# Two groups of gathered samples weighted by one multiply and summed by one sum

## The chip, the cores and the metric

One core of one Trainium2 chip runs the whole program in one launch. The metric is the device time in microseconds, the median of three runs. The core has TensorE (PE, matmuls, with its own queue for weight loads), VectorE (DVE), ScalarE (ACT), GpSimd (POOL) and SyncE (SP), which issues most transfers. Each engine takes its instructions in program order; between engines they wait for each other's semaphores.

## The reference

The input `x` has shape (4, 256, 64, 64). Four residual layers follow one another, each `x = x + layer(group_norm(x))`. The change touches the first, a deformable convolution. Cut to that part:

```
G, P = 4, 9                      # groups of 64 channels, sampling points
xp     = inproj(y)               # the table that is sampled, padded by 6
offset = off(t); mask = softmax(mask_lin(t), over the 9 points of a group)
samp   = grid_sample(img, grid)  # 4 corners a point, bilinear
dout   = (samp * mask).sum(over the 9 points)
```

For each pixel and group 9 points x 4 corners = 36 vectors of 64 channels are fetched, each is multiplied by one weight (bilinear weight times mask), and the 36 are added up. The rest of layer 0 is 1x1 convolutions with a squeeze-and-excite gate. Layer 1 is a grouped convolution with rotated kernels, layer 2 linear attention with batch statistics, layer 3 a depthwise-like convolution with quantised weights.

## The kernel before

The four images (b = 0 to 3) go through stages: A (norm, first convolution, table, depthwise convolution, offsets, indices and weights), F (output projection and feed-forward), L1 and L2 (layers 1 and 2). L3, layer 3, comes last for all. The gathers of image b - 1 or b are spread as "units" over the stages that run meanwhile, in the order of the list `plan`.

An image has 32 tiles of 128 pixels (`TILES`), a tile 4 groups (`G`): 512 units in all. For a unit GpSimd issues nine indirect gathers (L430), each of 128 partitions x 4 corners x 64 channels, into one of four places of the buffer `ring`, one place a group. It waits for the semaphore `ring_free` (L426) before a unit: the place must have been summed in the tile before. VectorE's `unit` (L1491) waits for the nine gathers (`gathered0` to `gathered3`), multiplies the place by its weights in place (L1506), waits for that (`weighted`), adds up the 36 vectors into `dbuf` (L1512) and gives the place back. Ahead of a tile's first unit the tile's 144 weights are copied into PSUM (L1495) in the stretches called apart. In the others (the last F and the extra tiles there) the multiply is cut in four and takes its weights from `wt` in SBUF. A tile's `dbuf` is stored by SyncE when all four groups are summed (L490).

Where VectorE's units stand among its other work is fixed when the program is written. `Stream.begin` (L379) lists the units of a turn, `TURNS` says how many tiles a turn takes, `give` (L388) puts the next few at a place in the loop body, and `finish` (L393) the rest at its end. `extra` (L402) puts one whole tile between stages. The places that matter below are these:
- la, the first loop of L2 (L1976), gives two units at a time, four times a turn.
- lb, the second loop of L2 (L2032), gives one unit ahead of a chunk's wait for ScalarE (`bO`) and one behind the chunk. The loop of L1 (L1914) has the same form: two units at a time, but one where it runs as "L1 last".
- f1 (L1774), the first loop of F, gives two units ahead of its first chunk and one behind each chunk. f2 (L1816), the second, gives one unit behind each of eight steps.
- a1 (L1627) and a2 (L1661), the loops of A, give one unit at a time; the depthwise part of a2 gives one behind its fourth and eighth tap.

Stages are parted by barriers of all engines but GpSimd (L327). GpSimd goes on through them, as far as places are free.

Of the kernel before, what the change touches and what calls it, by code (L numbers as in the profile page):

```python
# [20 lines left out]
ALU = mybir.AluOpType  # L21
ACT = mybir.ActivationFunctionType
AX_X = mybir.AxisListType.X
# [5 lines left out]
P = 128  # L29
# [7 lines left out]
TILES = HW // P  # L37
G, K2 = 4, 9
GC = C // G
PTS = G * K2  # L40
CORNERS = 4
# [33 lines left out]
PARTS = 4  # L75
# [59 lines left out]
def network_kernel(nc, x, par, wa, wr, wf, wq, w3, out):  # L135
    ctx = ExitStack()
    with ctx:
        def sb(name, shape, dt=F32):
            return ctx.enter_context(nc.sbuf_tensor(name, shape, dt))
# [6 lines left out]
        def sem(name):  # L146
            if name not in sems:
                sems[name] = ctx.enter_context(nc.semaphore(name))
            return sems[name]
# [15 lines left out]
        ring = sb("ring", [P, G, K2 * CORNERS * GC])  # L165
        idx = sb("idx", [P, 2, TILES * PTS], U32)
        idx_stage = sb("idx_stage", [P, 2, 2 * PTS], U32)
        wt = sb("wt", [P, TILES * PTS * CORNERS])
        dbuf = sb("dbuf", [P, 4, C])
# [9 lines left out]
        wps = PS[:, 7, 0:PTS * CORNERS]  # L179
# [73 lines left out]
        def seg(t, start, n):  # L253
            return t[:, bass.ds(start, n)]
# [1225 lines left out]
        def _(dve):  # L1480
            vec = nc.vector
# [8 lines left out]

            def unit(b, t, g, j):  # L1491

                if g == 0:
                    if stream.apart:
                        vec.tensor_copy(wps, seg(wt, t * (PTS * CORNERS), PTS * CORNERS)).then_inc(sem("wt_moved"), 1)  # L1495
                        dve.wait_ge(sem("wt_moved"), t + (b * TILES + 1))
                    else:
                        dve.sem_inc(sem("wt_moved"), 1)
                dve.wait_ge(sem(f"gathered{g}"), t * (16 * K2) + 16 * K2 * (b * TILES + 1))
                parts = 1 if stream.apart else PARTS  # L1500
                n = K2 * CORNERS // parts
                for part in range(parts):
                    rg = ring[:, g, part * n * GC:(part + 1) * n * GC].rearrange("p (k c) -> p k c", c=GC)
                    weights = wps[:, g * n:(g + 1) * n] if stream.apart \
                        else seg(wt, t * (PTS * CORNERS) + (g * PARTS + part) * n, n)
                    last = vec.tensor_tensor(rg, rg, weights.unsqueeze(2).to_broadcast([P, n, GC]), ALU.mult)  # L1506
                last.then_inc(sem("weighted"), 1)
                dve.wait_ge(sem("weighted"), t * G + (b * TILES * G + g + 1))
                if g == 0:

                    dve.wait_ge(sem("d_stored"), t * 16 + (16 * b * TILES + 16 - 16 * j))
                vec.tensor_reduce(dbuf[:, j, g * GC:(g + 1) * GC], ring[:, g, :].rearrange("p (k c) -> p c k", c=GC),  # L1512
                                  AX_X, ALU.add).then_inc(sem("ring_free"), 1)

            stream = Stream(unit)

            def weights_for(gi, all_tiles=True):
# [772 lines left out]
```

## Time and profile before

| | us |
|---|---|
| runs, median (lowest to highest) | 6932.77 (6926.98 to 6935.47) |
| profiled execution | 6945.93 |
| its span | 6944.1 |
| VectorE busy | 5165.7 (74%) |
| GpSimd busy | 4465.9 (64%) |
| TensorE busy | 3732.4 (54%) |
| ScalarE busy | 1121.1 (16%) |

The span runs from the first instruction to the last; the profiled execution's own time has 1.8 us around it. Busy time leaves out what an engine spends on waits, branches and on issuing: GpSimd shows 64%, although its gathers follow one another closely for most of the span. What an engine waited for stands in brackets behind a row of the timeline.

### The profile page before, as it was taken

How to read it: one execution, taken by the hardware profiler on the slowest of the kernel's cores; microseconds unless marked ns; L12 is line 12 of the kernel's file. 1: busy time of each engine (PE TensorE's matmuls, PEld its weight loads, DVE VectorE, ACT ScalarE, POOL GpSimd, SP SyncE). 2: the span in 40 equal slices, each digit the busy share in tenths (PEclk: the TensorE clock that was granted, in tenths of full speed). 3: DMA queues.
4: the chain of work that ended last, by engine and by line, in shares of the span. 5: the costliest groups of instructions: out<-in, count | busy, mean ns of one | idle time of the engine just before them, and what ended most of it. 6: DMA issues, size and time to landing. Idle time of an engine off the chain costs nothing.

```text
span 6944.1 us, 44944 instructions
## 1 busy us (share of the span) xinstructions
PE 3732.4 (54%) x11426; PEld 1972.3 (28%) x11426; DVE 5165.7 (74%) x4213; ACT 1121.1 (16%) x1689; POOL 4465.9 (64%) x4677
## 2 busy tenths in 40 slices
PE   7243251351574526643874436536747654296969
PEld 4122121221232204421321124312223431143534
DVE  5879788797787768976787679867777996535545
ACT  2010100101111002221110012211110221111335
POOL 0777777777777777777777777777777777500000
PEclk9576675675787758866886668767878877698989
DMA  4463643644444333465443334564343446311048
GB/s 118 141 172 105 192 141 121 207 129 159 144 132 131 106 107 123 131 216 186 130 131 118 107 109 131 194 202 142 120 128 108 129 132 221 127 43 45 37 145 237
DMA packets 529912, 954.28 MB, mean 137 GB/s; under 512 B 268560, under 2 KB 325904, under 8 KB 513680
## 3 DMA queue, kind: packets, MB, share of 16 engines
q0 software_dynamic: 221184, 604.27, 27.9%
q1 hardware_dynamic: 308624, 348.78, 15.5%
q8 instruction: 46, 0.75, 0.0%
q14 instruction: 58, 0.48, 0.0%
HBM read 792.34 MB, written 160.37 MB: 137 GB/s over the span
## 4 chain that ended last, share of the span: by engine, by line
POOL 43%; issue 21%; DVE 15%; PE 13%; DMA 4%; ACT 2%; SPq 1%; DVEq 0%; POOLq 0%; ACTq 0%
POOL ring L430 43%; PE PS L791 13%; DVE ring L1506 5%; DVE dbuf L1512 2%; DMA ring<-table,idx_stage 1%; DMA img<-d_dram 1%; ACT img L1184 1%; DVE sm L1968 1%; DVE sm L1984 1%; DVE sm L1991 0%; DVE img L1937 0%; DVE img L1995 0%; DMA img<-q_dram 0%; SPq L678 0%; DVE wb_sb L2002 0%
## 5 line engine op out<-in xcount | busy, mean ns | idle before, releaser
L430 POOL DMA_INDIRECT ring<-table,idx_stage x4608 | 4442.7, 964 | 1414.8 <-issue 1372.3
L1512 DVE TENSOR_REDUCE dbuf<-ring 128x64 f32<-128x2304 f32 x512 | 2072.6, 4048 | 30.3 <-DMA d_dram<-dbuf 1.8
L791 PE MATMUL PS<-img,wb_sb 128*128 128x512 f32 (+1 forms) x3328 | 1655.7, 657 | 495.0 <-DVE img L1824 251.5
L1506 DVE TENSOR_TENSOR ring<-ring,PS 128x2304 f32<-128x2304 f32 x480 | 1224.4, 2551 | 605.5 <-DMA ring<-table,idx_stage 594.6
L791 PE MATMUL PS<-img,wa_sb 128*128 (+2 forms) x2848 | 842.7, 635 | 603.2 <-DVE img L1920 224.3
L791 PEld LDWEIGHTS PS<-img,wb_sb 128*128 128x128 f32 x3328 | 693.6, 213 | 1424.1 <-issue 1002.2
L791 PEld LDWEIGHTS PS<-img,wa_sb 128*128 128x128 f32 (+1 forms) x2848 | 368.9, 164 | 1047.5 <-issue 983.2
L473 POOL MEMSET img<- 128x6745 f32 x1 | 5.7, 5722 | 719.0 <-DMA o_dram<-img 719.0
L1184 ACT ACTIVATE img<-PS,sm 128x512 f32<-128x512 f32 x384 | 247.8, 680 | 1028.8 <-PE PS L791 1026.6
L791 PE MATMUL PS<-wa_sb,cb 128*128 128x108 f32 (+1 forms) x1024 | 239.3, 400 | 312.9 <-DVE cb L1575 250.4
L791 PE MATMUL PS<-sm,params 128*128 128x4 f32 x28 | 7.7, 350 | 726.9 <-DVE sm L1554 709.1
L888 PE MATMUL PS<-params,img 128*128 128x128 f32 x256 | 62.9, 427 | 543.1 <-DMA img<-d_dram 543.1
L791 PEld LDWEIGHTS PS<-wa_sb,cb 128*128 128x128 f32 x1024 | 214.9, 277 | 356.1 <-DVE cb L1575 262.3
L1184 ACT ACTIVATE img<-PS 128x512 f32<-128x512 f32 (+1 forms) x224 | 173.9, 777 | 718.5 <-PE PS L888 379.1
L1184 ACT ACTIVATE img<-img (+6 forms) x241 | 185.5, 772 | 615.9 <-PE PS L791 297.1
L1824 DVE SCALAR_TENSOR_TENSOR img<-PS,sm,img 128x512 f32<-128x512 f32 x256 | 179.3, 742 | 141.4 <-ACT img L1184 141.4
L1090 PE MATMUL PS<-params,img 128*128 128x128 f32 x512 | 108.3, 392 | 279.9 <-ACT img L1184 245.3
L791 PE MATMUL PS<-cb,img 128*128 128x256 f32 x1024 | 251.0, 395 | 2.0 <-ACT img L1184 2.0
L1184 ACT ACT_TABLE_LOAD x20 | 25.7, 1283 | 1349.2 <-DVE sm L1559 1348.3
L791 PE MATMUL PS<-wb_sb,img 128*128 128x512 f32 x512 | 230.8, 604 | 11.8 <-ACT img L1184 11.6
L791 PEld LDWEIGHTS PS<-sm,params 128*128 128x128 f32 x28 | 6.9, 312 | 734.7 <-issue 734.7
L888 PEld LDWEIGHTS PS<-params,img 128*128 128x128 f32 x256 | 50.2, 224 | 562.1 <-issue 532.7
(223 smaller groups left out, 3379.1 us busy)
## 6 DMA issues: line engine op xcount, KB each, us to landing
ring<-table,idx_stage POOLq DMA_INDIRECT x4608
table<-cb SPq DMA_DIRECT2D x64, 512.0 KB, 5.9
img<-y_dram SPq DMA_DIRECT2D x64, 512.0 KB, 6.4
q_dram<-img SPq DMA_DIRECT2D x32, 1024.0 KB, 4.3
img<-q_dram SPq DMA_DIRECT2D x32, 1024.0 KB, 8.5
img<-in_x SPq DMA_DIRECT2D x8, 2048.0 KB, 12.0
y_dram<-cb SPq DMA_DIRECT2D x64, 256.0 KB, 2.2
d_dram<-dbuf SPq DMA_DIRECT2D x128, 128.0 KB
```

What stands on the lines that cost most here:

```text
L430: nc.gpsimd.indirect_dma_start(out=ring[:, g, p * CORNERS * GC:(p + 1) * CORNERS * GC], out_offset=None, in_=tab[b], in_offset=bass.Indire ...
L473: nc.gpsimd.memset(img2[:, 0:FIRST[3]], 0.0).then_inc(sem("e_cleared"), 1)
L791: return nc.tensor.matmul(o, l, r, start=start, stop=stop, **kw)
L888: last = nc.tensor.transpose(PS[:, 2 * h + k, s * P:(s + 1) * P], i2[h][:, s * C + k * P:s * C + (k + 1) * P], v("ident"))
L1090: last = nc.tensor.transpose(PS[:, m, s * P:(s + 1) * P], QS[:, s * HID + m * P:s * HID + (m + 1) * P], v("ident"))
L1184: return nc.scalar.activation(o, i, f, **kw)
L1506: last = vec.tensor_tensor(rg, rg, weights.unsqueeze(2).to_broadcast([P, n, GC]), ALU.mult)
L1512: vec.tensor_reduce(dbuf[:, j, g * GC:(g + 1) * GC], ring[:, g, :].rearrange("p (k c) -> p c k", c=GC), AX_X, ALU.add).then_inc(sem("ring_ ...
L1824: last = vec.scalar_tensor_tensor(out=i2[6 + q % 2][:, half], in0=PS[:, 2 * (q % 2) + j, :], scalar=fb[:, 2 * q + j:2 * q + j + 1], in1=i2 ...
L1968: link(vec.tensor_reduce(cmax[:, s2], PS[:, s2, :], AX_X, ALU.max))
L1984: link(vec.tensor_reduce(mx, q3, AX_X, ALU.max))
```

## The change

`unit` on VectorE does nothing for groups 0 and 2. For groups 1 and 3 it waits for both gathers, that of the group before and its own, multiplies both places at once (128x4608, or eight instructions of 128x576 where weights come from SBUF), sums both at once into 128 values (two groups of 64) and raises `ring_free` by two. The semaphores' counts are set to match. GpSimd's code is the same: it asks for the same numbers, and the number for the first place of a pair now comes with that of the second.

```diff
@@ -1490,27 +1490,34 @@
 
             def unit(b, t, g, j):
 
-                if g == 0:
+                if g % 2 == 0:
+                    return
+                if g == 1:
                     if stream.apart:
                         vec.tensor_copy(wps, seg(wt, t * (PTS * CORNERS), PTS * CORNERS)).then_inc(sem("wt_moved"), 1)
                         dve.wait_ge(sem("wt_moved"), t + (b * TILES + 1))
                     else:
                         dve.sem_inc(sem("wt_moved"), 1)
-                dve.wait_ge(sem(f"gathered{g}"), t * (16 * K2) + 16 * K2 * (b * TILES + 1))
-                parts = 1 if stream.apart else PARTS
-                n = K2 * CORNERS // parts
-                for part in range(parts):
-                    rg = ring[:, g, part * n * GC:(part + 1) * n * GC].rearrange("p (k c) -> p k c", c=GC)
-                    weights = wps[:, g * n:(g + 1) * n] if stream.apart \
-                        else seg(wt, t * (PTS * CORNERS) + (g * PARTS + part) * n, n)
-                    last = vec.tensor_tensor(rg, rg, weights.unsqueeze(2).to_broadcast([P, n, GC]), ALU.mult)
+                for h in (g - 1, g):
+                    dve.wait_ge(sem(f"gathered{h}"), t * (16 * K2) + 16 * K2 * (b * TILES + 1))
+                both = ring[:, g - 1:g + 1, :]
+                n = K2 * CORNERS
+                if stream.apart:
+                    rg = both.rearrange("p g (k c) -> p (g k) c", c=GC)
+                    last = vec.tensor_tensor(rg, rg, wps[:, (g - 1) * n:(g + 1) * n].unsqueeze(2).to_broadcast([P, 2 * n, GC]), ALU.mult)
+                else:
+                    n = n // PARTS
+                    for part in range(2 * PARTS):
+                        rg = both.rearrange("p g c -> p (g c)")[:, part * n * GC:(part + 1) * n * GC].rearrange("p (k c) -> p k c", c=GC)
+                        weights = seg(wt, t * (PTS * CORNERS) + ((g - 1) * PARTS + part) * n, n)
+                        last = vec.tensor_tensor(rg, rg, weights.unsqueeze(2).to_broadcast([P, n, GC]), ALU.mult)
                 last.then_inc(sem("weighted"), 1)
-                dve.wait_ge(sem("weighted"), t * G + (b * TILES * G + g + 1))
-                if g == 0:
+                dve.wait_ge(sem("weighted"), t * 2 + (b * TILES * 2 + g // 2 + 1))
+                if g == 1:
 
                     dve.wait_ge(sem("d_stored"), t * 16 + (16 * b * TILES + 16 - 16 * j))
-                vec.tensor_reduce(dbuf[:, j, g * GC:(g + 1) * GC], ring[:, g, :].rearrange("p (k c) -> p c k", c=GC),
-                                  AX_X, ALU.add).then_inc(sem("ring_free"), 1)
+                vec.tensor_reduce(dbuf[:, j, (g - 1) * GC:(g + 1) * GC].rearrange("p (g c) -> p g c", g=2),
+                                  both.rearrange("p g (k c) -> p g c k", c=GC), AX_X, ALU.add).then_inc(sem("ring_free"), 2)
 
             stream = Stream(unit)
```

On VectorE, at the start of lb, the second loop of L2, before (L1512 gives one place back, L2038 waits for ScalarE's `bO`):

```order
L2024 COPY wb_sb<-PS 64x4x64
...
L1495 COPY PS<-wt 128x144
...
L1506 TENSOR_TENSOR ring<-ring,PS 128x2304 [waits gathered0]
...
L1512 TENSOR_REDUCE dbuf<-ring 128x64 [waits d_stored]
...
L2038 ISA [waits bO]
L2038 BN_STATS ostats<-PS 128x6
...
L2038 BN_STATS ostats<-PS 128x6
...
L2042 SCALAR_TENSOR_TENSOR img,lm<-img,lm,PS 128x512
...
L2042 SCALAR_TENSOR_TENSOR img,lm<-img,lm,PS 128x512
L1506 TENSOR_TENSOR ring<-ring,PS 128x2304 [waits gathered1]
...
L1512 TENSOR_REDUCE dbuf<-ring 128x64 [waits weighted]
```

The same place after:

```order
L2031 COPY wb_sb<-PS 64x4x64
...
L2045 ISA [waits bO]
L2045 BN_STATS ostats<-PS 128x6
...
L2045 BN_STATS ostats<-PS 128x6
...
L2049 SCALAR_TENSOR_TENSOR img,lm<-img,lm,PS 128x512
...
L2049 SCALAR_TENSOR_TENSOR img,lm<-img,lm,PS 128x512
...
L1497 COPY PS<-wt 128x144
...
L1507 TENSOR_TENSOR ring<-ring,PS 128x4608 [waits gathered1,gathered0]
...
L1519 TENSOR_REDUCE dbuf<-ring 128x128 [waits d_stored]
```

The first group's weight copy, multiply and sum stood ahead of the chunk's work and of its wait for `bO`. Now nothing of the units stands there; the weight copy and the pair come behind the chunk.

On VectorE, in f2, the second loop of F, before (L1824 is a step of the feed-forward):

```order
L1824 SCALAR_TENSOR_TENSOR img<-PS,sm,img 128x512 [waits gD]
...
L1495 COPY PS<-wt 128x144
...
L1506 TENSOR_TENSOR ring<-ring,PS 128x2304 [waits gathered0]
...
L1512 TENSOR_REDUCE dbuf<-ring 128x64 [waits d_stored]
...
L1824 SCALAR_TENSOR_TENSOR img<-PS,sm,img 128x512 [waits gD]
...
L1506 TENSOR_TENSOR ring<-ring,PS 128x2304 [waits gathered1]
...
L1512 TENSOR_REDUCE dbuf<-ring 128x64 [waits weighted]
...
L1824 SCALAR_TENSOR_TENSOR img<-PS,sm,img 128x512 [waits gD,gZ]
...
L1506 TENSOR_TENSOR ring<-ring,PS 128x2304 [waits gathered2]
...
L1512 TENSOR_REDUCE dbuf<-ring 128x64 [waits weighted]
```

The same place after (the step's line is L1831):

```order
L1831 SCALAR_TENSOR_TENSOR img<-PS,sm,img 128x512 [waits gD]
...
L1831 SCALAR_TENSOR_TENSOR img<-PS,sm,img 128x512 [waits gD]
...
L1497 COPY PS<-wt 128x144
...
L1507 TENSOR_TENSOR ring<-ring,PS 128x4608 [waits gathered1,gathered0]
...
L1519 TENSOR_REDUCE dbuf<-ring 128x128 [waits d_stored]
...
L1831 SCALAR_TENSOR_TENSOR img<-PS,sm,img 128x512 [waits gD,gZ]
...
L1831 SCALAR_TENSOR_TENSOR img<-PS,sm,img 128x512 [waits gD,gZ]
...
L1507 TENSOR_TENSOR ring<-ring,PS 128x4608 [waits gathered3,gathered2]
...
L1519 TENSOR_REDUCE dbuf<-ring 128x128 [waits weighted]
```

Groups and steps took turns one by one. Now two steps follow each other, and then a pair.

## Rows read from the trace of the kernel before

**Rows 1.** The page: engines' busy time; shares of the chain that ended last.
```profile
PE 3732.4 (54%) x11426; PEld 1972.3 (28%) x11426; DVE 5165.7 (74%) x4213; ACT 1121.1 (16%) x1689; POOL 4465.9 (64%) x4677
...
POOL 43%; issue 21%; DVE 15%; PE 13%; DMA 4%; ACT 2%; SPq 1%; DVEq 0%; POOLq 0%; ACTq 0%
```

**Rows 2.** The page's costliest groups: busy us, mean ns, then idle before.
```profile
L430 POOL DMA_INDIRECT ring<-table,idx_stage x4608 | 4442.7, 964 | 1414.8 <-issue 1372.3
L1512 DVE TENSOR_REDUCE dbuf<-ring 128x64 f32<-128x2304 f32 x512 | 2072.6, 4048 | 30.3 <-DMA d_dram<-dbuf 1.8
...
L1506 DVE TENSOR_TENSOR ring<-ring,PS 128x2304 f32<-128x2304 f32 x480 | 1224.4, 2551 | 605.5 <-DMA ring<-table,idx_stage 594.6
```

**Rows 3.** Who waited for whom: us in total, times, longest us.
```profile
POOL ring L430 <- issue: 1372.3, 4499, 1.1
...
DVE ring L1506 <- DMA ring<-table,idx_stage: 627.4, 192, 9.0
...
POOL ring L430 <- DVE dbuf L1512: 30.4, 48, 3.6
```

**Rows 4.** Line L430: ns min/median/max, first and last start us.
```profile
L430 POOL DMA_INDIRECT ring<-table,idx_stage x4608: 943/949/1996, 158.5 to 6031.3; - x192
```

**Rows 5.** Groups of VectorE's instructions by shape, for other sizes.
```profile
L1995 DVE TENSOR_TENSOR img<-img,sm 128x512 f32<-128x512 f32 x128 | 80.7, 692 | 1.1
...
L1991 DVE TENSOR_REDUCE sm<-img 128x32 f32<-128x2048 f32 x32 | 72.9, 2278 | 9.0 <-ACT img L1184 9.0
```

**Rows 6.** Timeline, start of la (image 0): start us, duration us, [idle before].
```profile
2599.89 0.95 POOL L430 DMA_INDIRECT ring<-table,idx_stage  x1 [0.30 <-issue]
...
2602.56 2.56 DVE L1506 TENSOR_TENSOR ring<-ring,PS 128x2304 f32<-128x2304 f32 x1 [4.66 <-DMA ring<-table,idx_stage]
2605.15 4.00 DVE L1512 TENSOR_REDUCE dbuf<-ring 128x64 f32<-128x2304 f32 x1
...
2625.08 1.23 DVE L1968 TENSOR_REDUCE sm<-PS 128x2 f32<-128x1024 f32 x1 [8.92 <-PE PS L791]
...
2644.43 4.14 DVE L1512 TENSOR_REDUCE dbuf<-ring 128x64 f32<-128x2304 f32 x1
...
2649.38 0.95 POOL L430 DMA_INDIRECT ring<-table,idx_stage  x1 [3.26 <-DVE dbuf L1512]
...
2651.07 4.10 DVE L1512 TENSOR_REDUCE dbuf<-ring 128x64 f32<-128x2304 f32 x1
```

**Rows 7.** Timeline, start of lb (image 0).
```profile
2993.29 2.55 DVE L1506 TENSOR_TENSOR ring<-ring,PS 128x2304 f32<-128x2304 f32 x1
...
3011.54 1.30 DVE L2038 BATCH_NORM_STATS2 ostats<-PS 128x512 f32 x2 [11.55 <-ACT img L1184]
...
3013.22 0.95 POOL L430 DMA_INDIRECT ring<-table,idx_stage  x1 [0.30 <-issue]
...
3016.66 4.10 DVE L1512 TENSOR_REDUCE dbuf<-ring 128x64 f32<-128x2304 f32 x1
```

**Rows 8.** Timeline, start of f2 (image 0).
```profile
1870.51 4.10 DVE L1512 TENSOR_REDUCE dbuf<-ring 128x64 f32<-128x2304 f32 x1
...
1873.87 0.94 POOL L430 DMA_INDIRECT ring<-table,idx_stage  x1 [0.30 <-issue]
```

**Rows 9.** Timeline, start of a1 (image 3).
```profile
1274.13 0.95 POOL L430 DMA_INDIRECT ring<-table,idx_stage  x1 [0.30 <-issue]
...
1275.51 4.08 DVE L1512 TENSOR_REDUCE dbuf<-ring 128x64 f32<-128x2304 f32 x1
```

**Rows 10.** Timeline, f1 for image 3, beside the last gathers.
```profile
5986.03 1.35 POOL L430 DMA_INDIRECT ring<-table,idx_stage  x1 [2.28 <-DVE dbuf L1512]
...
5987.93 4.00 DVE L1512 TENSOR_REDUCE dbuf<-ring 128x64 f32<-128x2304 f32 x1
```

**Rows 11.** Two tiles of a2, two of f2: length, engines' busy us, clock, DMA.
```profile
554.00:641.00 87.00, 43.11 (x136) 22.41 (x134) 84.39 (x63) 5.64 (x9) 66.45 (x69) 0.74 0.34 106
2027.00:2117.00 90.00, 64.93 (x125) 27.07 (x124) 71.51 (x46) 10.13 (x16) 68.49 (x73) 0.85 0.42 131
```

## Prediction, made before the changed kernel ran

> **What bounds the kernel now.** The page's first lines come first: VectorE is the busiest engine, yet GpSimd heads the chain of waits with 43%, and the 21% called issue stands beside it [rows 1]. So VectorE's busy share is no bound by itself. The costliest groups say what GpSimd does: 4608 gathers of 964 ns [rows 2]. Next, GpSimd's own waits: 1372.3 us went to "issue" between gathers and only 30.4 us, in 48 waits, to VectorE giving places back, the longest 3.6 us; VectorE in its turn waited 627.4 us, 192 times, for gathered samples [rows 3]. The first gather starts at 158.5 us and the last at 6031.3 us [rows 4]. In between GpSimd never rests: 4442.7 + 1372.3 = 5815 us over 512 groups is 11.36 us a group (11.3 where nothing disturbs it: nine times 0.95 + 0.30). The time is therefore a start of 158.5 us, GpSimd's gathers, and about 913 us behind the last one. A change on VectorE counts only where it makes GpSimd wait, or stops it waiting; of the latter there are just 30.4 us.
>
> **What a pair saves.** Today a group costs 2.551 + 4.048 = 6.6 us [rows 2], two cost 13.2. A plain multiply of 512 elements takes 0.692 us [rows 5], one of 2304 2.551, so an element costs 1.04 ns and an instruction 0.16 us: 4608 elements are 2.551 + 2304 x 1.04 ns = 4.95 us, 0.15 less than two. The sum keeps its elements and access pattern, with one more outer step. Another sum over 2048 elements, 2.278 us [rows 5], has about 0.15 us above 1.04 ns an element, so I take 2 x 4.048 - 0.15 = 7.95. A pair is then 12.9 us: 0.3 saved, 256 x 0.3 = 77 us of VectorE time. Ends: nothing saved, or 0.6 a pair (nothing known excludes a slower sum either; each 1 us more on it counts in the late pair ahead of a place and in the pair at the place, 2 x 19 = 38 us by the sum below, and more where VectorE has little room). All of this hides behind GpSimd unless VectorE is late.
>
> The Trainium skill (Perfetto Trace Analysis, "Optimizing Scalar/DVE Operations") gives about 60 ns of overhead per VectorE instruction on SBUF, and says that grouping helps "if the engine is saturated", while an engine that is not saturated but causes bubbles elsewhere is better served by breaking instructions up. By its figure the saving is 512 x 0.06 = 31 us instead of 77. Whether VectorE counts as saturated is what the waits of [rows 3] decide: they say no, and then the second half of that rule speaks against this change.
>
> **What it costs: the place comes back later.** The ring has four places. Now GpSimd may refill a place as soon as its own group is summed; after, the first two come back together. Two things make the first place late.
> First, in place: a group that is used to be released first must wait for its neighbour. Where VectorE keeps up this is harmless: gathered samples arrive 1.7 us after the last gather ends (2599.89 + 0.95 to 2602.56, [rows 6]); 1.7 + 12.9 + 0.8 us is 15.4, and GpSimd meanwhile has two groups, 22.6 us, to gather. The 0.8 is what a released place needs to be seen (2644.43 + 4.14 to 2649.38 [rows 6]).
> Second, in time: where VectorE waits for gathers, it used to do the first group while the second was on its way. Now it starts both when the second is there, and ends at 2602.56 + 13.0 = 2615.5 instead of 2605.15 + 4.00 = 2609.15 [rows 6]: 6.4 us late. If loop work follows, 7 us of slack swallow it (22.6 - 15.4). If a change of stage follows, with barriers and chains through the other engines, everything moves 6.4 us.
>
> So at each start of a stage that VectorE enters late, GpSimd's new stall over its old start is: end of the second group's sum before, + 6.4 late, - 0.3 saved, + 0.8 to be seen, - start of the gather that needs the first place. That is **R + 6.9 - G**. Since G is the real start, waits of before are taken off. GpSimd has no reserve, so each such stall is paid once in full. Place by place:
> - Start of L2's first loop (la), three times. R = 2651.07 + 4.10 = 2655.2, G = 2649.4 [rows 6]: 12.7 us. Three make 38.
> - Start of L2's second loop (lb), three times, and of the loop "L1 last", once. Here the first group also moves: it was summed ahead of a wait of 11.55 us for ScalarE, and the order now puts it behind. R = 3016.66 + 4.10 = 3020.8, G = 3013.2 [rows 7]; with 6.6 us for the group that loses its cover: 3020.8 + 6.9 + 6.6 - 3013.2 = 21.1 us. The four lie between 20.3 and 21.1: 83.
> - Starts of F's second loop, three times: R = 1874.6, G = 1873.9 [rows 8]: 7.6. The three starts of F's first loop for the images 0 to 2 and the start of A for image 2 are of this kind, seven in all, 6.8 to 8.2: 53.
> - The start of A's first loop for image 3: R = 1275.51 + 4.08 = 1279.6, G = 1274.1 [rows 9]: 12.4.
> - F's first loop for image 3, with the last gathers, where VectorE never waits for gathers again and one burst counts, at its last place: R = 5991.9, G = 5986.0 [rows 10]: 12.8.
> - Starts of A's second loop, three times. VectorE is busy for 84.39 of 87 us there [rows 11], so it makes up lateness only slowly. By the same count about 2 us each: 6.
>
> Sum: 38 + 83 + 53 + 12 + 13 + 6 = 205 us at 19 places. The steady loops I cost at nothing. In A's second loop the second group's sum keeps its place in the order, and two tiles take VectorE 87 us where GpSimd needs eight groups, 90.4. In F's second loop VectorE is busy for 71.51 of 90 us [rows 11], so 4.6 us a group are free, enough for a pair that starts late and runs 6.4 us longer in one piece. If that cover is gone, the third rival below applies. Behind the last gather nothing changes but the last pair, under 7 us, which in the trace VectorE already owes there.
>
> SyncE's stores wait for all four groups, which come at the same point, and its queue is not late: it waits on VectorE already. GpSimd's instructions, PE's and ScalarE's are the same in number and order. The wait on the previous store moves from the first group to the pair, later, so it costs nothing. Behind the pair's wait for gathers stands now, on VectorE, up to 13 us of work that PE and ScalarE cannot get past; that is the 6.4 us above.
>
> The profiled execution took 6945.9 us: 6944.1 of span and 1.8 around it. With 205 it is 7151. The median of the runs shown, 6932.8, is 13 us lower, so the forecast is **7138 us**, 3.0% slower.
>
> **Rivals.**
> 1. The lateness is swallowed. At these places VectorE waits for PE (8.92 us at the start of la, [rows 6]) or ScalarE (11.55, [rows 7]); if those engines are late for reasons of their own, 6.4 us vanish there. For it: these are real waits. Against: barriers stand ahead of them, and the chain comes back to VectorE's own last instruction. At the 16 places before the loops of A2 all swallowed: 16 x 6.4 = 102 less, about 7036; with the moved group's 26 us too, 7010.
> 2. Not slower. GpSimd would have to find the pair in time everywhere, because VectorE runs far ahead at stage starts. Then the 77 us saved could at most pay back the 30.4 us of waits and pull in serial stretches: 6933 - 30 = 6903, or, were VectorE the bound throughout, 6933 - 77 = 6856. The point of decision: R + 0.5 below G without any lateness. R is beyond G by 5 to 8 us in [rows 6, 7, 9, 10], so those stall even without lateness; only in [rows 8] is it under 1 us.
> 3. More is lost. The group that moves behind a body step loses its cover in the steady loops as well, or the sum with the extra dimension runs slower. Six starts of F loops and three of A2 at 6.6 or less give 40 to 55: 7178 to 7193; a sum 1 us slower gives 38: 7176. Both give some 7200 to 7230.
> 4. The change doesn't do what it says: had the pair form not applied in one of the two kinds of stretches (weights in PSUM or not), less would be lost. The order shows the wide multiply and sum everywhere in the gathers' stretches, so I give this nothing.
>
> **How the numbers follow.** Forecast as worked out (about 7105 to 7175): 0.62. Swallowed in part or whole: 0.17. More lost: 0.17. Not slower: 0.04, half of it no change. Within 0.2%, 14 us, a measurement of this kernel tells no difference. The likeliest case's own range is 7105 to 7175. Most of the two neighbours is taken in for 8 of 10: 7060 to 7210. Chances: faster 0.02, same 0.02, slower 0.96.
>
> **What will show it.** Multiply 128x4608 near 4.95 us and sum 128x128 near 7.95. GpSimd's waits on the sum rise from 30 us to about 235, in waits of 7 to 21 us at the stage starts, not spread over the loops; gathers still 1.25 us apart otherwise, and the last near 6237 us with about 913 us behind it. VectorE's waits for gathers grow in all, since GpSimd is the bound. Wrong would be: waits of GpSimd in the middle of F2 or A2 (rival 3); waits for PE or ScalarE at stage starts shorter by 6 us (rival 1); a tail that changes.

## The result, and the profile after

The median went from 6934.12 us (6926.98 to 6935.88) to **7201.97 us** (7197.66 to 7206.18), four runs each: a ratio of 1.0387 with a 95% interval of 1.0372 to 1.0403. The change costs 268 us, 3.9%. The profiled execution took 7200.61 us with a span of 7198.8, which is 254.7 us above the span of before.

The page of after, answering [rows 1, 2]: busy time, the chain that ended last, and the costliest groups (busy us, mean ns, idle before).

```profile
PE 3688.4 (51%) x11426; PEld 1953.2 (27%) x11426; DVE 5097.1 (71%) x3717; ACT 1121.3 (16%) x1689; POOL 4451.5 (62%) x4677
...
POOL 37%; issue 20%; DVE 20%; PE 15%; DMA 5%; ACT 2%; SPq 1%; DVEq 0%; POOLq 0%; ACTq 0%
...
L430 POOL DMA_INDIRECT ring<-table,idx_stage x4608 | 4429.5, 961 | 1692.2 <-issue 1408.2
L1519 DVE TENSOR_REDUCE dbuf<-ring 128x128 f32<-128x4608 f32 x256 | 2028.0, 7922 | 37.2 <-DVE ring L1507 20.5
...
L1507 DVE TENSOR_TENSOR ring<-ring,PS 128x4608 f32<-128x4608 f32 x240 | 1188.8, 4953 | 811.5 <-DMA ring<-table,idx_stage 803.6
```

VectorE got nearly what was promised: it is busy for 68.6 us less, 5165.7 to 5097.1. A pair costs 4.953 + 7.922 = 12.88 us instead of 13.20. The gathers are as many and as long as before. Yet the kernel is slower, because the idle time ahead of L430 rose from 1414.8 us [rows 2] to 1692.2, by 277 us. The waits say for whom (us in total, times, longest us), against [rows 3]:

```profile
POOL ring L430 <- issue: 1408.2, 4474, 19.0
...
DVE ring L1507 <- DMA ring<-table,idx_stage: 803.6, 148, 12.2
...
POOL ring L430 <- DVE dbuf L1519: 271.5, 71, 21.4
```

GpSimd's wait for the sum went from 30.4 us to 271.5. "issue" rose by 36 us, with a longest wait of 19.0 us where it was 1.1: these are two waits of 18.9 and 19.0 us at the starts of lb for images 0 and 1, where GpSimd stands at `ring_free` and the profile named no releaser (the first is shown below). VectorE waits more for gathers too, 803.6 us against 627.4: it has to wait for two groups at once, and the group that it used to do meanwhile is no longer there to fill the time. Each engine waits longer for the other; that is what a coarser handshake looks like. Line L430, against [rows 4]:

```profile
L430 POOL DMA_INDIRECT ring<-table,idx_stage x4608: 940/946/1986, 159.5 to 6295.4; - x192
```

The last gather starts 264.1 us later than before (6031.3), and 903.4 us follow it instead of 912.8. So all of the loss lies in the gathers' stretch, and the tail gave 9.4 us back.

The start of la for image 0, against [rows 6] (start us, duration us, idle before):

```profile
2697.24 4.96 DVE L1507 TENSOR_TENSOR ring<-ring,PS 128x4608 f32<-128x4608 f32 x1 [6.72 <-DMA ring<-table,idx_stage]
2702.30 7.84 DVE L1519 TENSOR_REDUCE dbuf<-ring 128x128 f32<-128x4608 f32 x1
...
2725.75 1.23 DVE L1975 TENSOR_REDUCE sm<-PS 128x2 f32<-128x1024 f32 x1 [8.61 <-PE PS L791]
...
2747.63 8.04 DVE L1519 TENSOR_REDUCE dbuf<-ring 128x128 f32<-128x4608 f32 x1 [0.21 <-DVE ring L1507]
...
2756.49 0.94 POOL L430 DMA_INDIRECT ring<-table,idx_stage  x1 [15.91 <-DVE dbuf L1519]
```

The sum ends at 2755.67, and GpSimd starts again 0.82 us later, after 15.91 us of nothing. Before, it waited 3.26 us here; 12.6 more. The wait for PE is as long as it was (8.61 against 8.92), so nothing of the late start was swallowed.

The start of lb for image 0, against [rows 7]:

```profile
3122.02 1.30 DVE L2045 BATCH_NORM_STATS2 ostats<-PS 128x512 f32 x2 [22.06 <-ACT img L1184]
...
3130.22 7.90 DVE L1519 TENSOR_REDUCE dbuf<-ring 128x128 f32<-128x4608 f32 x1 [0.21 <-DVE ring L1507]
...
3138.91 0.94 POOL L430 DMA_INDIRECT ring<-table,idx_stage  x1 [18.90 <-issue]
```

The wait for ScalarE grew from 11.55 us to 22.06. The 2.55 + 4.0 us of a group and its weight copy used to stand ahead of it and now stand behind it, and the wait at the barrier, which in before stood ahead of that copy, is now part of it:

```profile
2992.86 0.31 DVE L1495 COPY PS<-wt 128x144 f32 x1 [5.32 <-ACTq L338]
```

11.55 + 5.32 + 0.3 + 6.6 is 23.8, about 2 us more than the 22.06 measured. GpSimd pays 18.90 us where it paid nothing.

Stage by stage, in us from one start of gathers to the next; in brackets stands the image that the stage works on (for L1 last the image that is gathered). A row runs from the first gather for group 3 of a stage's first tile to the same of the next stage, so that the stall for the second tile counts in its stage; e5 to e7 are experiments below.

| stage (image) | before | after | e5 | e6 | e7 |
|---|---|---|---|---|---|
| a1 (1) | 185.3 | 193.6 | 188.5 | 195.5 | |
| a2 (1) | 233.2 | 243.1 | 234.5 | 241.0 | |
| start of A (2) | 45.3 | 51.4 | 47.4 | 51.4 | |
| a1 (3) | 185.0 | 195.3 | 199.5 | 196.0 | |
| f1 (0) | 181.0 | 193.3 | 188.9 | 193.0 | |
| f2 (0) | 411.0 | 424.0 | 414.5 | 423.7 | |
| L1 (0) | 361.5 | 361.5 | 360.8 | 361.4 | |
| la (0) | 366.8 | 379.4 | 375.4 | 395.4 | 384.0 |
| lb (0) | 136.2 | 154.5 | 150.7 | 137.8 | 147.8 |
| L1 last (3) | 180.7 | 201.3 | 195.0 | 181.1 | 180.3 |

L1's normal loop, eight tiles with two groups given at a time, loses nothing at all.

### The profile page after: what moved, and what is told of

The parts are those of the page before. It is cut to its first block, busy times and chain, and to the rows that moved or that the text cites. A ratio compares the mean times of both kernels' runs of the same rounds, so it can differ in the third digit from the quotient of the medians.

```text
span 7198.8 us, 44662 instructions
## 1 busy us (share of the span) xinstructions
PE 3688.4 (51%) x11426; PEld 1953.2 (27%) x11426; DVE 5097.1 (71%) x3717; ACT 1121.3 (16%) x1689; POOL 4451.5 (62%) x4677
## 4 chain that ended last, share of the span: by engine, by line
POOL 37%; issue 20%; DVE 20%; PE 15%; DMA 5%; ACT 2%; SPq 1%; DVEq 0%; POOLq 0%; ACTq 0%
POOL ring L430 36%; PE PS L791 14%; DVE dbuf L1519 7%; DVE ring L1507 6%; DMA ring<-table,idx_stage 2%; DMA img<-d_dram 1%; ACT img L1184 1%; DVE PS L1661 1%; DVE ring L1513 1%; DVE stats L1577 0%; DVE img L1944 0%; DMA img<-q_dram 0%; DVE cb L1909 0%; DVE sm L1975 0%; SPq L678 0%
## 5 line engine op out<-in xcount | busy, mean ns | idle before, releaser
L430 POOL DMA_INDIRECT ring<-table,idx_stage x4608 | 4429.5, 961 | 1692.2 <-issue 1408.2
L1519 DVE TENSOR_REDUCE dbuf<-ring 128x128 f32<-128x4608 f32 x256 | 2028.0, 7922 | 37.2 <-DVE ring L1507 20.5
L791 PE MATMUL PS<-img,wb_sb 128*128 128x512 f32 (+1 forms) x3328 | 1636.2, 653 | 577.9 <-DVE img L1831 276.2
L1507 DVE TENSOR_TENSOR ring<-ring,PS 128x4608 f32<-128x4608 f32 x240 | 1188.8, 4953 | 811.5 <-DMA ring<-table,idx_stage 803.6
L1831 DVE SCALAR_TENSOR_TENSOR img<-PS,sm,img 128x512 f32<-128x512 f32 x256 | 175.6, 741 | 143.1 <-ACT img L1184 143.1
```

The source lines that it names most:

```text
L430: nc.gpsimd.indirect_dma_start(out=ring[:, g, p * CORNERS * GC:(p + 1) * CORNERS * GC], out_offset=None, in_=tab[b], in_offset=bass.Indire ...
L791: return nc.tensor.matmul(o, l, r, start=start, stop=stop, **kw)
L1507: last = vec.tensor_tensor(rg, rg, wps[:, (g - 1) * n:(g + 1) * n].unsqueeze(2).to_broadcast([P, 2 * n, GC]), ALU.mult)
L1519: vec.tensor_reduce(dbuf[:, j, (g - 1) * GC:(g + 1) * GC].rearrange("p (g c) -> p g c", g=2), both.rearrange("p g (k c) -> p g c k", c=GC) ...
L1831: last = vec.scalar_tensor_tensor(out=i2[6 + q % 2][:, half], in0=PS[:, 2 * (q % 2) + j, :], scalar=fb[:, 2 * q + j:2 * q + j + 1], in1=i2 ...
```

## The experiments

**Which chip.** Three chips were used. On the first, before took 6930.83 us (seven runs) beside e5 to e8. Its time is that of the result above, so e5 to e8 are compared with after's 7202 too. On the two others the same kernel took 8614.57 us (beside e1 to e4) and 8628.33 or 8618.69 us (beside e9 to e12). Each ratio is against before on the same chip, and what sets the time on the two others is in the last section: GpSimd isn't what bounds it there. The expectations were all worked out for the first chip.

Theory A is the prediction's: GpSimd is the bound, the first place comes back late, and VectorE's late start at a stage's beginning is paid in full. Its three parts are the return in pairs, the joint wait for both gathers, and the first group's move behind a piece of the body. The rivals were that the wide instructions themselves or one of these parts alone did it.

**e1_release2**: before, with both places returned at the second sum. Waits and instructions stay.

```diff
-      AX_X, ALU.add).then_inc(sem("ring_free"), 1)
+      AX_X, ALU.add).then_inc(sem("ring_free" if g % 2 else "sum_done"), 2 if g % 2 else 1)
```

> Single multiplies and sums at their old places in the order, but a place is given back only with its neighbour (ring_free raised by 2 at the second sum). Theory A (the late return of the first place costs, and the late start doubles it): slower than before by 60 to 90 us, 73 worked out from before's rows by carrying each start of a stage forward, all of it as waits of GpSimd at the starts of la, lb, f1, f2. Theory B (the wide instructions themselves or the joint wait do it, the return in pairs is hidden by the ring's slack): no change, 6934.

8878.8 us, ratio 1.0311 (1.0287 to 1.0335). The return in pairs alone costs 3.1% there, 264 us instead of the 60 to 90 expected, with not one instruction changed in size. It isn't all at the starts of stages either. By stage, against e3 on the same chip, whose total is 0.2% above before's, this kernel loses 15 to 32 us in each f2, 10 to 17 in each la and 11 to 14 in each lb, and gets 9 to 11 back in L1. Why the price is so much higher there is open.

**e2_moved**: before, with both single groups at the second one's place, each with its own wait and return.

```diff
-            def unit(b, t, g, j):
+            def one(b, t, g, j):
...
+            def unit(b, t, g, j):
+                if g % 2:
+                    one(b, t, g - 1, j)
+                    one(b, t, g, j)
```

> Single multiplies and sums, each with its own wait and its own return, but both at the second group's place in the order. Only the move of the first group is left. Theory A: slower by 30 to 50 us, 39 worked out, at the starts of lb and L1 last (about 6 us each) and at the starts of f1, f2 and a2. Rival: the move is harmless, since GpSimd's slack of 22 us a pair covers 6.6 us: within 10 us of before.

8818.27 us, 1.0232 (1.0206 to 1.0257). The move alone costs as well, 204 us there where 30 to 50 were expected.

**e3_joint_wait**: before, but a pair's first group waits for both groups' gathers.

```diff
-  dve.wait_ge(sem(f"gathered{g}"), ...)
+  for h in ((g, g + 1) if g % 2 == 0 else (g,)):
+      dve.wait_ge(sem(f"gathered{h}"), ...)
```

> As before, but the first group of a pair waits for the gathers of both; order, single instructions and single returns as before. Only the late start is left. Theory A: VectorE ends its last pair ahead of a change of stage 6.5 us later, 79 us slower in all (60 to 95). Rival (lateness is swallowed by the other engines' waits at the stage starts): under 25 us.

8635.16 us, 1.0023 (1.0005 to 1.0041). Next to nothing there: 21 us, as the rival had it, and not 79. Its waits suggest why:

```profile
PE PS L791 <- issue: 1683.0, 337, 71.8
POOL ring L430 <- DVE dbuf L1513: 1655.4, 167, 41.2
...
DVE ring L1507 <- DMA ring<-table,idx_stage: 175.6, 30, 9.3
```

VectorE waited for gathers 30 times, 175.6 us, not 192 times and 627.4 us as in before on the first chip [rows 3], and GpSimd waited 1655.4 us for VectorE. A joint wait can cost only where VectorE arrives before the samples. So this run agrees with theory A's condition and says nothing of its price on the first chip.

**e4_two_sums**: after, with two sums of 128x2304, each returning its place.

```diff
-  vec.tensor_reduce(dbuf[:, j, (g - 1) * GC:(g + 1) * GC]..., both..., ...).then_inc(sem("ring_free"), 2)
+  for h in (g - 1, g):
+      vec.tensor_reduce(dbuf[:, j, h * GC:(h + 1) * GC], ring[:, h, :]..., ...).then_inc(sem("ring_free"), 1)
```

> The changed kernel with its joint wait and its multiply of 128x4608, but two sums of 128x2304, each giving its own place back. The first place is back 4 us earlier than with one sum, the second 0.1 later. Theory A: about 4 us less stall at each of the 20 places where GpSimd waits for the first of a pair, 85 us faster than the changed kernel: 7115 (7095 to 7140), about 180 slower than before. If only the number of instructions counted, it would be 0 to 10 us slower than the changed kernel: 7202 to 7212.

8866.82 us, 1.0285 (1.0247 to 1.0323), 252 us more than before there. Since the wide multiply needs both groups, the first place still comes back late and the first group is still moved. After itself wasn't run on this chip, so what the separate return gives back there stays open.

**e5_moved_release2**: before with the move of e2 and the return of e1. The instructions and their waits for gathers stay single; what after has beyond it is the joint wait and the wide instructions.

```diff
-            def unit(b, t, g, j):
+            def one(b, t, g, j):
...
-      AX_X, ALU.add).then_inc(sem("ring_free"), 1)
+      AX_X, ALU.add).then_inc(sem("ring_free" if g % 2 else "sum_done"), 2 if g % 2 else 1)
+
+            def unit(b, t, g, j):
+                if g % 2:
+                    one(b, t, g - 1, j)
+                    one(b, t, g, j)
```

> Both groups at the second one's place in the order and both places returned together, but single instructions and single waits. Theory A: move and return in pairs together, slower than before by 122 us (105 to 145): about 7056. What is left to the changed kernel's 7202 is the joint wait less the saving of the wide instructions. If the wide instructions themselves were the cost, this kernel would be near before, under 40 us slower.

7080.92 us on the first chip, 1.0214 (1.0197 to 1.0231): +150 us, a little above the range expected. GpSimd's wait for the sum:

```profile
POOL ring L430 <- DVE dbuf L1512: 159.2, 57, 16.2
```

So 150 of the 268 us are the move and the return in pairs. The other 118 us come with the joint wait and the wide instructions together. The instructions are by themselves 0.32 us a pair shorter, so the cost is put down to the joint wait; no run on this chip has that wait alone. By the prediction's rule, a start that is 6.4 us late with 0.3 saved, at 19 places, makes 19 x 6.1 = 116. The total agrees, but in part by luck, for the places do not agree one by one: beyond e5, la and lb lose 4 us, f2 9.5 and the first a2 8.6, while a1 of image 3 gains 4.

**e6_pair_first**: after, with the pair ahead of the body's wait in la, lb and L1 last.

```diff
@@ L1 last
-                        stream.give(1, 4)
+                        stream.give(1, 2 if gi == B - 1 else 4)
@@ la
+                        stream.give(1, 4)
                         for half in range(2):
...
-                        stream.give(1, 4)
@@ lb
-                        stream.give(1, 4)
+                        stream.give(1, 2)
```

> The changed kernel, with the pair put ahead of the waits for PE and ScalarE: in la ahead of the wait for the queries, in lb and in L1 last ahead of the chunk's wait. Theory A: the stall at the start of la falls from 12.5 us to under 4, those at the starts of lb and L1 last from 19 to 21 to under 3: 34 + 72 less, 7202 - 106 = 7096 (7075 to 7130). Rival (the stalls come from what GpSimd or the transfers do at a change of stage): no change, 7202.

7204.16 us, 1.0398 (1.038 to 1.0415). The total missed the expectation by 108 us, but two effects of opposite sign stand in it, and the table parts them. Where the first group got its cover back, lb and L1 last, the stages return to the time of before: 154.5 to 137.8 and 201.3 to 181.1, together 72 us over the four, as expected. In la it went the other way: 379.4 to 395.4, some 51 us in three images instead of a gain of 34. The starts of f1 lost another 19, so that gains and losses cancel. VectorE's wait for PE at la's first operation shows it, in after and then in e6:

```profile
DVE sm L1975 <- PE PS L791: 60.8, 22, 8.8
```

```profile
DVE sm L1975 <- PE PS L791: 125.6, 64, 9.4
```

22 waits became 64: every one of them. (Of the 22, 16 belong to image 3, whose la has no groups; in the other three 6 became 48.) In la ScalarE's exponential needs VectorE's subtraction, VectorE needs its result, and the next half follows through TensorE. Work placed ahead of the subtraction holds up the whole ring of engines in each pass. The group that I put there was cover in its old place, behind the subtraction.

**e7_la_first**: before, with only that move in la, to see the effect by itself.

```diff
+                        stream.give(1, 4)
                         for half in range(2):
...
-                        stream.give(1, 4)
```

> The kernel before, with the two groups that la takes first put ahead of the wait for the queries. GpSimd's waits at the three starts of la (3.3 + 1.8 us each) should go: 15 us faster, 6920 (6912 to 6930) by theory A, that GpSimd is the bound wherever it does not wait. If la is bound by VectorE and PE instead, their chain starts 13 us later: up to 40 us slower.

7013.61 us, 1.0116 (1.0099 to 1.0133): +83 us from moving one line, with no instruction changed. The same waits, in before and then in e7:

```profile
DVE sm L1968 <- PE PS L791: 63.5, 22, 9.5
```

```profile
DVE sm L1968 <- PE PS L791: 126.5, 64, 9.5
```

And two passes of e7's la, on VectorE:

```profile
2655.82 1.23 DVE L1968 TENSOR_REDUCE sm<-PS 128x2 f32<-128x1024 f32 x1 [1.51 <-PE PS L791]
2659.26 1.23 DVE L1968 TENSOR_REDUCE sm<-PS 128x2 f32<-128x1024 f32 x1 [1.53 <-PE PS L791]
...
2704.30 1.23 DVE L1968 TENSOR_REDUCE sm<-PS 128x2 f32<-128x1024 f32 x1 [1.50 <-PE PS L791]
2707.74 1.22 DVE L1968 TENSOR_REDUCE sm<-PS 128x2 f32<-128x1024 f32 x1 [1.29 <-PE PS L791]
```

A pass takes 48.5 us here. In before the same two passes have no wait for PE:

```profile
2662.32 1.23 DVE L1968 TENSOR_REDUCE sm<-PS 128x2 f32<-128x1024 f32 x1
...
2705.11 1.23 DVE L1968 TENSOR_REDUCE sm<-PS 128x2 f32<-128x1024 f32 x1
```

There VectorE's pass took 42.8 us and GpSimd's four groups 45.2, so GpSimd was the slower. With a pass of 48.5 us la changes its bound from GpSimd to the chain through three engines. lb takes longer too (136.2 to 147.8 us). la lost 48 us in the three images and lb 34. Between the two profiled executions the other stages gave 9 us back and the tail behind the last gather grew by 7.5, so that the spans differ by 81; neither was traced. The expected 6920 us, by theory A as it stood, was wrong, and its warning of up to 40 us was too low: where a group stands can make another chain the bound.

**e8_before_six**: before, with six gathers a group instead of nine; the other twelve of the 36 vectors are set to zero once and not fetched.

```diff
+NG = 6
...
-                for p in range(K2):
+                for p in range(NG):
...
+                vec.memset(ring[:, :, NG * CORNERS * GC:], 0.0)
```

> The kernel before with six gathers a group instead of nine (three of nine points are left out: what stands at their places is set to zero once). GpSimd needs 7.5 us a group instead of 11.3 and is no longer the bound in the dense loops. Expected 6200 to 6400 us: 512 x 3 x 1.25 = 1925 us less would be 5010, but VectorE and PE stop it long before. If GpSimd were no bound now, the time would stay at 6934.

6304.23 us, 0.9096 (0.9081 to 0.9112): 627 us less for a third fewer gathers, with VectorE's work as before. So the gathers bound the kernel. Fewer gathers also mean fewer transfers, so this run alone doesn't part GpSimd's issuing from the transfers; the trace of before points to the issuing, since gathers follow each other 1.25 us apart while their queue takes 27.9% of the 16 DMA engines' span. There is a limit too: 1536 gathers of 1.25 us are 1920 us, and only a third of that came back, since the bound passes to VectorE. Its page (busy, chain, the gathers' group):

```profile
PE 3669.3 (58%) x11426; PEld 1944.2 (31%) x11426; DVE 5153.3 (82%) x4214; ACT 1120.5 (18%) x1689; POOL 2981.5 (47%) x3141
...
DVE 42%; issue 25%; PE 23%; DMA 4%; ACT 2%; SPq 1%; DVEq 1%; ACTq 0%; PEldq 0%
...
L431 POOL DMA_INDIRECT ring<-table,idx_stage x3072 | 2958.9, 963 | 2223.6 <-DVE dbuf L1513 1257.4
```

VectorE now heads the chain, where GpSimd did with 43% [rows 1].

**e9_after_six**: after, with the same third of the gathers left out.

```diff
+NG = 6
...
-                for p in range(K2):
+                for p in range(NG):
...
+                vec.memset(ring[:, :, NG * CORNERS * GC:], 0.0)
```

> The changed kernel with six gathers a group (three of nine points are left out, as in e8, which took 6304 us). GpSimd now waits for VectorE 1257 us in e8, so VectorE is the bound over long stretches. Theory A: the 0.3 us saved a pair now count, up to 77 us; against them stand the starts of stages, where the late return costs less because GpSimd is ahead: net 10 to 60 us faster than e8, 6245 to 6295. If the pair form is worse in itself, it is as much slower than e8 as the changed kernel is than before: 6304 + 268 = 6570.

6884.6 us against 8618.69, 0.7997 (0.7957 to 0.8036), on another chip than e8. The comparison that it was made for, e9 against e8 where VectorE is the bound, needs the same chip. It stays open.

**e10_release2_again** and **e11_joint_wait_again**: the kernels of e1 and e3 once more, on the third chip. The edits are those of e1 and e3.

> [...] With before at 6931: theory A, places returned in pairs alone, slower by 73 us (60 to 95), all at the starts of stages, and half of e5's 150. Theory B (return in pairs is hidden by the slack): under 15.

> [...] Theory A, the late start alone: slower by 79 us (60 to 100). Together with e5 (150 us slower: move and return in pairs) it should then leave for the changed kernel's 268 some 39 us, which is the saving of the wide instructions with its sign turned plus what the late start gains from the other two. Rival (lateness swallowed): under 25.

8889.06 us, 1.0303 (1.0271 to 1.0334), and 8628.82 us, 1.0013 (0.9992 to 1.0034). Both repeat the result of e1 and e3, e10 also by stage against e11, and neither gives the price on the first chip. There the joint wait's share rests on the difference between after and e5 alone.

**e12_lb_pair_first**: after, with the pair first in lb and L1 last only, the part of e6 that worked.

```diff
-                        stream.give(1, 4)
+                        stream.give(1, 2 if gi == B - 1 else 4)
...
-                        stream.give(1, 4)
+                        stream.give(1, 2)
```

> The changed kernel with the pair ahead of the chunk's wait in lb and in L1 last only; la stays. In e6 these four places gave back 72 us and la, changed too, took 51. Expected: 7202 - 72 = 7130 (7115 to 7150). If the gain of e6 at lb was only what its longer la had pushed there, it stays above 7180.

9029.81 us against 8618.69, 1.0483 (1.0448 to 1.0518), on the third chip, where after has no time of its own. Its lb took 166 to 171 us against 175 to 181 in e11 on the same chip, and its L1 last 228.8 against 239.8, so the places that it changes are short; what makes it longer stands elsewhere. Whether this version gives 7130 us on the first chip is open. By e6's places it would still be 3% slower than before. No run points to a version that beats before.

## Why the prediction held, and where it was off

**The bound was read rightly.** The chain and the two waits [rows 1, 3] said that GpSimd sets the time and VectorE, though busier, does not. e8 shows it: fewer gathers, less time, same VectorE work.

**What a pair saves was right**: 4.95 and 7.95 us forecast, 4.953 and 7.922 measured, 0.32 us a pair, some 80 us in all by these durations (VectorE's busy time fell by 68.6), and it is hidden. The Trainium skill (Perfetto Trace Analysis, "Optimizing Scalar/DVE Operations") says that grouping can help a saturated engine and that breaking up may help where an engine causes bubbles on others. The trace agrees with the second half in its direction: grouping cost 268 us, 150 of them without any wider instruction (e5). The same section's figure of about 60 ns for each VectorE instruction on SBUF is engine-busy time, and it says that profiled durations show about twice that; an estimate by that page is then some 120 ns. Here an instruction less saved 149 ns at the multiply (2 x 2551 - 4953), which reads its weights from PSUM, and 174 ns at the sum (2 x 4048 - 7922). The 31 us that the prediction worked out from the 60 ns were therefore too low.

**The rule held where the order stayed.** GpSimd's gathers, after against before, in us of new stall:

| place | forecast | measured |
|---|---|---|
| la, 3 | 38 | 12.6 + 12.4 + 12.3 = 37 |
| lb, 3, and L1 last | 83 | 18.6 + 18.7 + 18.7 + 21.0 = 77 |
| f2, 3 | 24 | 12.5 + 12.4 + 11.9 = 37 |
| f1, 3 | 22 | 12.8 + 12.4 + 11.1 = 36 |
| a1 of image 3 | 12 | 12 |
| a1 of images 1 and 2 | 0 | 8.3 + 12.3 = 21 |
| starts of A, images 2 and 3 | 8 | 6.2 + 5.9 = 12 |
| a2, 3 | 6 | 10.5 + 8.4 + 8.7 = 28 |
| last f1 | 13 | 14 |
| first gathers | 0 | 3 |

The measured column makes 276; steps of up to 2.4 us back leave 264. At a1 of image 3 the agreement is luck. The rule without the joint wait (6.1 us less) gives 6.3 us there, but e5, which has no joint wait, loses 15.5. The first group lost its cover here too, which the forecast didn't count; VectorE waits for `cb` in e5, and 7.58 us in after, but not in before:

```profile
1286.82 1.23 DVE L1580 SCALAR_TENSOR_TENSOR cb<-cb 128x1024 f32<-128x1024 f32 x1 [8.62 <-ACT cb L1184]
```

In after this and the late start didn't add up.

The steady loops cost nothing, as forecast, and GpSimd's waits are few and long: 71, of up to 21.4 us. One figure of that forecast was misread: the 18.5 us that VectorE has free in two tiles of f2 [rows 11] are 2.3 us a group and 4.6 a pair, not 4.6 a group.

**What was mis-sized** is the term for the starts of F, 6.8 to 8.2 us each, and of a2, 2 each, with a1 of images 1 and 2 at nothing. I charged a moved group for its lost cover at lb and L1 last alone, and left the same effect at the other starts to the third rival, at 40 to 55 us. It happened: f1 and f2 hold some 27 us more than forecast and a2 22. In f1 nearly all of it stands at the second pair of the stage (5.0, 4.7 and 3.7 us), where the forecast counted the first pair only. The 21 us at a1 of images 1 and 2 are of two kinds. By the rule image 1 should pay 341.06 + 6.9 - 347.1 = 0.9 and image 2 811.89 + 6.9 - 810.2 = 8.6 (in before the second group's sum ended at 341.06 and 811.89); the second is a place that I overlooked. The other 7.4 and 3.7 us I put down to lost cover again. The start of A for image 3 (5.9) and the first gathers (3) I overlooked too. At a1 of image 2, in after:

```profile
832.88 1.23 DVE L1582 SCALAR_TENSOR_TENSOR cb<-cb 128x1024 f32<-128x1024 f32 x1 [7.71 <-ACT cb L1184]
...
834.51 4.96 DVE L1507 TENSOR_TENSOR ring<-ring,PS 128x4608 f32<-128x4608 f32 x1 [0.19 <-DVE PS L1497]
839.67 7.85 DVE L1519 TENSOR_REDUCE dbuf<-ring 128x128 f32<-128x4608 f32 x1 [0.21 <-DVE ring L1507]
...
848.33 1.14 POOL L430 DMA_INDIRECT ring<-table,idx_stage  x1 [12.16 <-DVE dbuf L1519]
```

and there in before:

```profile
797.28 2.55 DVE L1506 TENSOR_TENSOR ring<-ring,PS 128x2304 f32<-128x2304 f32 x1
799.97 4.10 DVE L1512 TENSOR_REDUCE dbuf<-ring 128x64 f32<-128x2304 f32 x1
804.10 1.23 DVE L1575 SCALAR_TENSOR_TENSOR cb<-cb 128x1024 f32<-128x1024 f32 x1
```

The first group used to fill the time in which ScalarE makes `cb`. Now VectorE idles for 7.71 us and does the whole pair afterwards. In the whole run this wait doubled, from 35.9 us to 72.7.

Lost cover alone doesn't make the 22 us of a2. At its start for image 1 the second step on `cb` waits for ScalarE in e5 and in after alike, and not in before:

```profile
516.67 1.22 DVE L1580 SCALAR_TENSOR_TENSOR cb<-cb 128x1024 f32<-128x1024 f32 x1 [5.31 <-ACT cb L1184]
```

```profile
533.39 1.23 DVE L1582 SCALAR_TENSOR_TENSOR cb<-cb 128x1024 f32<-128x1024 f32 x1 [4.77 <-ACT cb L1184]
```

Yet e5's a2 is 1.3 us longer than before's and after's 9.9. I take it that the slack which nearly hid the lost cover in e5 was gone in after, where the pair starts late as well. The two effects together make the 22 us, and no run parts them.

At f2 the lateness of 7.6 us became 12.5 in two steps. At the end of f1 in after:

```profile
1906.05 1.39 DVE L1789 SCALAR_TENSOR_TENSOR img<-PS,params,img 128x512 f32 x2
1913.26 1.41 DVE L1789 SCALAR_TENSOR_TENSOR img<-PS,params,img 128x512 f32 x2 [5.81 <-PE PS L791]
1914.59 4.94 DVE L1507 TENSOR_TENSOR ring<-ring,PS 128x4608 f32<-128x4608 f32 x1
...
1948.72 1.41 DVE L1831 SCALAR_TENSOR_TENSOR img<-PS,sm,img 128x512 f32<-128x512 f32 x2 [7.56 <-ACT img L1184]
1952.16 1.41 DVE L1831 SCALAR_TENSOR_TENSOR img<-PS,sm,img 128x512 f32<-128x512 f32 x2 [2.02 <-ACT img L1184]
...
1967.93 0.94 POOL L430 DMA_INDIRECT ring<-table,idx_stage  x1 [12.86 <-DVE dbuf L1519]
```

Two pieces of the body now stand next to each other, with no group between them; the second waits 5.81 us for PE, and the last pair starts about 3.0 us after its samples had come (in before that group's multiply started at 1830.06, plus the 81.5 us by which gathers were late by then, is 1911.6). At f2 the second piece waits 2.02 us for ScalarE. 7.6 + 3.0 + 2.0 is 12.6.

At lb the forecast was 2 us too high each: VectorE came to its first chunk 3.4 us late, not 6.4 (3122.02 - 3011.54 is 110.5, and gathers stood 107.1 late). At its copy into `wb_sb`, its last work ahead of that chunk, it was still 5.3 us late (3099.11 - 2986.67 is 112.4), so 2 of the 3 us vanished between there and the chunk, in the wait for ScalarE. That is the first rival, in small; at la it didn't occur.

**The tail** gave 9.4 us back, where I expected nothing. VectorE owed a little more than three groups there in before, and its last sum ended 21.6 us behind the last gather's end; in after it is 15.3 us. I put that down to the stalls of GpSimd in the last f1, in which VectorE caught up. The rest of the 9.4 us wasn't traced. And the profiled execution of before was 12 us above its median, that of after 1 us below: hence 255 us between the spans and 268 between the medians.

The sum was 205 where 268 was measured. The mechanism was the forecast's; a little under a quarter of the loss, some 60 us (27 + 22 + 7.4 + 3.7), was the third rival's, lost cover at the starts of stages, partly together with the late start. 7202 us lies outside the 7105 to 7175 that the prediction gave for its likeliest case and 8 us inside its outer bound of 7210, which took in most of that rival.

## What to carry to other kernels

When a producer is the bound and a ring buffer joins it to the consumer, count what a wider instruction does to the ring: the first place comes back one whole instruction pair later, and the consumer starts one group later. In a steady loop slack swallows this; at a change of stage most or all of it is paid, so count the stage starts. And when a piece of work is moved, ask at every one of its places which wait it used to fill: one line moved in la cost 83 us with nothing else changed.

## What the runs showed of the hardware

The same kernel took 6930.83 us on one chip and 8614.57 and 8628.33 us on two others. The instructions are not longer there: e11 differs from before by its joint wait alone, and VectorE is busy for 5159.3 us in it, against 5165.7 in before on the first chip, with 4043 ns for a sum against 4048. e11's waits, the longest sums:

```profile
PEld PS L791 <- issue: 4737.6, 5246, 127.1
PE PS L791 <- issue: 1693.4, 314, 126.9
POOL ring L430 <- DVE dbuf L1513: 1644.2, 169, 39.8
POOL ring L430 <- issue: 1465.3, 4423, 21.7
ACT img L1184 <- remote: 1352.4, 83, 42.1
```

TensorE waited 1693.4 us in 314 stretches of up to 126.9 us for nothing that the profile names; before on the first chip has no such row for PE. "remote" stands for another core or an unknown queue; 28% of e11's chain that ended last is put down to these, and none of before's. The mean granted clock of TensorE was 0.708 against 0.759, and TensorE also waited more. What holds back TensorE there stays open. It matters for reading a ratio: an edit whose price depends on who is the bound (the joint wait, 0.1 to 0.2% there and some 118 us here) can have a different price on another chip.

The wide sum over 36 vectors takes 1.72 ns an element (7922 ns for 4608), the wide multiply 1.07 (4953 ns). The 2304 elements added to an instruction cost 3874 ns at the sum and 2402 at the multiply, so one doubled instruction takes 0.17 and 0.15 us less than two.
